# A residual graph kernel: attention as fp16 products on 64x64 tiles, graph sums kept in PSUM, and a mix of three float32r products

## The chip, the cores and the metric

One core of one Trainium2 chip. The metric is the device time of one execution in microseconds, as the median of the runs.

## The reference, cut to what matters

The input is x, 128 batches of 64 rows of 512 float32, and one 64x64 graph `adj` for all batches.

```python
# L0: rows of a batch are mixed by the graph
x = layernorm(x + einsum('bnf,nm->bmf', x, adj * adj) + bias)
# L1: two graphs from two projections, then attention with both
z_l, z_g, v = h @ W_lang.T, h @ W_grav.T, h @ W_V.T          # h is the x above
A_l = relu(zn @ zn.T) * not_eye                  # zn: rows of z_l, normalised
A_g = exp(-max(sq_i + sq_j - 2 z_g @ z_g.T, 0) / (2 sigma**2)) * not_eye
K = w * row_stochastic(A_l * adj) + (1 - w) * row_stochastic(A_g * adj)
out = layernorm(h + (K @ v) @ W_O.T)
```

The result must be close to float32, so the kernel writes most products as three fp16 products (high x high, high x low, low x high).

## The kernel before, in words

The 128 batches are worked in 16 groups of 8 batches (512 rows, as 4 pairs of batches on 128 partitions). All engines run the same software pipeline, written out by hand: one turn handles group g, the group before it (`before`) and the one after it (`nxt`). Turn 0 and turn 15 stand outside the hardware loop, which holds two turns. Each engine runs its own list in order; semaphores join them. I call the start of a turn the moment at which TensorE begins `mix(nxt, 0)`.

TensorE's list in a turn is: `mix` of pairs 0 and 1 of the next group; `project` 0 (12 products); `mix` 2 and 3; `project` 1; `kernel_t` of the group before; `project` 2; four `attend`; `project` 3 to 7; `values` 0; `gram`; `values` 1; `symmetrise`; `values` 2; `spread`; `values` 3. `project` j fills one of three banks; ScalarE rounds it to fp16 (`p_high`, tile `p_hi`) and VectorE takes the rest (`p_low`, tile `p_lo`). From j = 3 on `project` j waits for `p_low` of j - 3.

VectorE's list begins with `similarities` and `gravities` of the group before, then `add_bias` 0 and 1 (tile `y`), `row_factors`, `p_low` 0, `scale_rows` (tile `ks_sb`, which `kernel_t` waits for), `add_bias` 2 and 3, two `row_stats`, `p_low` 1, `row_moments`, four `residual` (tile `o`), `p_low` 2, `norm_rows` (four times tile `h`), and the other `p_low`. ScalarE's list begins with `p_high` 0, `p_high` 1, `kt_copy`, `p_high` 2, three `h_high`, `p_high` 3. GpSimd computes both `rstd`, half of `h_lo`, and `t_diag`.

SyncE issues the loads of `x_in` and the stores of `o` in one queue, in order: a store waits for `out_ready`, which the last `normalise` of the group (tile `o`, ScalarE) completes. Of `x_in` there are two buffers; the load into one waits for the `mix` that read it.

At the end of a turn the graph sums run over VectorE: `sums` adds `ps_t` and `t_sb`, `distances` makes three more passes, and then ScalarE takes the exponential:

```python
dve.tensor_tensor(s_sb[:, :], ps_t[:, :], t_sb[:, :], ALU.add)
...
act.activation(e_sb[GR, :], w_sb[GR, :], ACT.Exp, scale=cexp[GR, 0:1])
```

Of the kernel before, what the change touches and what calls it, by code (L numbers as in the profile page):

```python
# [23 lines left out]
F16 = mybir.dt.float16  # L24
ALU = mybir.AluOpType
# [29 lines left out]
def resnorm_graph_kernel(nc, x, adj, bias, w_lang, w_grav, w_v, w_o, gate, log_sigma, out):  # L55
# [18 lines left out]
    with ctx:  # L74
# [10 lines left out]
        x_in = [sb(f"x_in{i}", [P, PAIRS, D]) for i in range(2)]  # L85
# [8 lines left out]
        u = sb("u", [P, PAIRS, D])  # L94
# [4 lines left out]
        v_diag = sb("v_diag", [P, ROWS])  # L99
        s_sb = sb("s_sb", [P, ROWS])  # L100
        w_sb = sb("w_sb", [P, ROWS])
# [3 lines left out]
        kt = sb("kt", [P, PAIRS, P])  # L105
# [13 lines left out]
        vec = sb("vec", [P, GB])  # L119
# [8 lines left out]
        w_raw["v"] = u  # L128
# [11 lines left out]
        ones_lg = sb("ones_lg", [P, P])  # L140
# [5 lines left out]
        wmix = sb("wmix", [P, P])  # L146
        not_eye = sb("not_eye", [P, N])
# [9 lines left out]
        cexp = sb("cexp", [P, 1])  # L157
        minus_half = sb("minus_half", [P, GB])
# [6 lines left out]
        t_scale = sb("t_scale", [P, 1])  # L165
        wv_scale = sb("wv_scale", [P, 1])
# [7 lines left out]
        ku_bank = [ps_k, *front, ps_k]  # L174
# [43 lines left out]
        u_ready = sem("u_ready")  # L218
# [18 lines left out]
        kt_ready = sem("kt_ready")  # L237
# [87 lines left out]
        def _(pe):  # L325
# [16 lines left out]
            def project(g, j, first):  # L342
# [15 lines left out]
                for n, (k, a, b) in enumerate(passes):  # L358
# [61 lines left out]
            def attend(g, p, mixed):  # L420
# [6 lines left out]
                elif p == 3:  # L427
                    pe.wait_ge(sum_ready, g.count(4, 1))
# [692 lines left out]
```

## Time and profile before

| what | value |
|---|---|
| median of 3 runs | 627.45 us (626.82 to 627.95) |
| span of the profiled execution | 625.0 us |
| median less span | 2.45 us |
| TensorE busy | 614.2 us, 98% of the span |
| VectorE, ScalarE, GpSimd busy | 444.2, 242.7, 155.5 us |
| share of the chain that ended last on TensorE | 96% |
| turns 2 and 3 | start at 112.70 and 148.44 us |

The profile gives the profiled execution by its span; a time of its own with what lies around the span is not in it, and the 2.45 us between the span and the median are taken as that. A busy time is the union of an engine's instructions. A TensorE record of 128x512 fp16 lasts 0.38 us though the next starts 0.216 us later: products overlap, so costs on TensorE are read from starts. A float32 product leaves two records.

### The profile page before, as it was taken

How to read it: one execution, taken by the hardware profiler on the slowest of the kernel's cores; microseconds unless marked ns; L12 is line 12 of the kernel's file. 1: busy time of each engine (PE TensorE's matmuls, PEld its weight loads, DVE VectorE, ACT ScalarE, POOL GpSimd, SP SyncE). 2: the span in 40 equal slices, each digit the busy share in tenths (PEclk: the TensorE clock that was granted, in tenths of full speed). 3: DMA queues.
4: the chain of work that ended last, by engine and by line, in shares of the span. 5: the costliest groups of instructions: out<-in, count | busy, mean ns of one | idle time of the engine just before them, and what ended most of it. 6: DMA issues, size and time to landing. Idle time of an engine off the chain costs nothing.

```text
span 625.0 us, 11961 instructions
## 1 busy us (share of the span) xinstructions
PE 614.2 (98%) x4468; PEld 315.0 (50%) x4468; DVE 444.2 (71%) x940; ACT 242.7 (39%) x413; POOL 155.5 (25%) x159
## 2 busy tenths in 40 slices
PE   9999999999999999999999999999999999999994
PEld 6543545454454545454454545445454545545452
DVE  1759486877868586876868687786858788686564
ACT  2345224333443424434432433344342443443333
POOL 1002205032231403123230503223140312323021
PEclk9999999999999999999999999999999999999999
DMA  8722203434123342423223342312334242302103
GB/s 269 244 44 87 51 1 68 136 53 125 52 62 116 64 134 60 141 42 87 90 50 134 67 134 55 120 51 58 119 67 134 59 143 42 92 17 51 69 2 135
DMA packets 89392, 55.05 MB, mean 88 GB/s; under 512 B 70816, under 2 KB 70816, under 8 KB 89376
## 3 DMA queue, kind: packets, MB, share of 16 engines
q1 hardware_dynamic: 19744, 38.05, 17.9%
q10 hardware_dynamic: 69632, 16.79, 13.4%
q8 instruction: 10, 0.16, 0.1%
q14 instruction: 6, 0.05, 0.0%
HBM read 21.27 MB, written 16.78 MB: 61 GB/s over the span
## 4 chain that ended last, share of the span: by engine, by line
PE 96%; DVE 2%; ACT 1%; POOL 0%; issue 0%; POOLq 0%; ACTq 0%; DVEq 0%
PE proj L359 31%; PE proj L375 27%; PE front L339 9%; PE ps_t L389 7%; PE front L429 4%; PE ps_k L429 4%; PE ps_t L400 3%; PE ps_v L409 2%; PE proj L499 2%; PE proj L529 2%; PE ps_v L416 2%; PE ps_t L499 1%; PE ps_k L329 1%; DVE p_lo L736 1%; PE ps_t L529 1%; DVE y L709 0%
## 5 line engine op out<-in xcount | busy, mean ns | idle before, releaser
L557 ACT ACTIVATE p_hi<-proj 128x512 f16<-128x512 f32 x128 | 75.9, 593 | 118.2 <-PE proj L359 117.7
L736 DVE TENSOR_TENSOR p_lo<-proj,p_hi 128x512 f16<-128x512 f32 x128 | 86.0, 688 | 20.9 <-ACT p_hi L557 17.9
L375 PE MATMUL proj<-m_hi,ht_hi 128*128 128x512 f16 x256 | 97.2, 380 | 0.7 <-DVE p_lo L736 0.7
L375 PE MATMUL proj<-m_hi,ht_lo 128*128 128x512 f16 x256 | 97.0, 379 | 0.0
L375 PE MATMUL proj<-m_lo,ht_hi 128*128 128x512 f16 x256 | 97.0, 379 | 0.0
L1026 POOL TENSOR_TENSOR ve<-mv,eps_ln 128x4 f32<-128x4 f32 x31 | 6.6, 212 | 307.7 <-DVE mv L718 211.5
L562 ACT ACTIVATE u<-proj 128x512 f32<-128x512 f32 x64 | 37.9, 592 | 82.7 <-PE proj L375 82.5
L543 ACT ACTIVATE h_hi<-h 128x512 f16<-128x512 f32 x64 | 36.5, 619 | 69.0 <-DVE h L726 69.0
L1065 POOL TENSOR_TENSOR h_lo<-h,h_hi 128x512 f16<-128x512 f32 x30 | 41.5, 1403 | 84.4 <-ACT h_hi L543 84.4
L359 PE MATMUL proj<-ht_hi,l_grav_hi 128*128 128x512 f16 x160 | 60.6, 379 | 0.6 <-DVE p_lo L736 0.6
L359 PE MATMUL proj<-ht_hi,l_lang_hi 128*128 128x512 f16 x160 | 60.8, 380 | 0.0
L359 PE MATMUL proj<-ht_lo,l_grav_hi 128*128 128x512 f16 x160 | 60.6, 379 | 0.0
L359 PE MATMUL proj<-ht_hi,l_grav_lo 128*128 128x512 f16 x160 | 60.6, 379 | 0.0
L359 PE MATMUL proj<-ht_lo,l_lang_hi 128*128 128x512 f16 x160 | 60.6, 379 | 0.0
L359 PE MATMUL proj<-ht_hi,l_lang_lo 128*128 128x512 f16 x160 | 60.6, 379 | 0.0
L339 PE MATMUL front<-x_in,wmix 128*128 128x512 f32 x128 | 60.2, 593 | 0.0
L593 ACT ACTIVATE o<-o,nmr,rstd 128x512 f32<-128x512 f32 x60 | 46.9, 807 | 9.7 <-issue 9.3
L709 DVE TENSOR_TENSOR y<-front,bias_b 128x512 f32<-128x512 f32 x64 | 42.5, 686 | 11.3 <-PE front L339 10.8
L389 PE MATMUL ps_t<-ht_hi,p_lo 128*128 128x64 f16 x512 | 46.5, 193 | 0.0
L389 PE MATMUL ps_t<-ht_lo,p_hi 128*128 128x64 f16 x512 | 46.5, 193 | 0.0
L389 PE MATMUL ps_t<-ht_hi,p_hi 128*128 128x64 f16 x512 | 46.5, 193 | 0.0
L389 PEld LDWEIGHTS ps_t<-ht_hi,p_hi 128*128 128x128 f16 x512 | 45.1, 98 | 2.3 <-issue 0.5
(166 smaller groups left out, 1051.8 us busy)
## 6 DMA issues: line engine op xcount, KB each, us to landing
x_in<-in_x SPq DMA_DIRECT2D x16, 1024.0 KB, 7.1
out<-o SPq DMA_DIRECT2D x15, 1024.0 KB, 5.0
w_raw_lang<-in_L_gnn_W_lang SPq DMA_DIRECT2D x4, 256.0 KB, 3.1
o<-in_L_gnn_W_O SPq DMA_DIRECT2D x1, 1024.0 KB, 10.2
w_raw_grav<-in_L_gnn_W_grav SPq DMA_DIRECT2D x4, 256.0 KB, 10.1
u<-in_L_gnn_W_V SPq DMA_DIRECT2D x1, 1024.0 KB, 12.0
ht_hi<-h_hi ACTq DMA_TRANSPOSE x64, 2.4
ht_lo<-h_lo ACTq DMA_TRANSPOSE x64, 2.5
```

The costliest lines, as they stand in the source:

```text
L339: pe.matmul(front[p % 2][:, :], wmix[:, :], x_in[g.parity][:, p, :], start=True, stop=True).then_inc(l0_done, 1)
L359: mm = pe.matmul(proj[j % 3][:, :], a[s][:, blk(k, c), :], b[g.parity][:, k, :], start=(n == 0), stop=(n == len(passes) - 1))
L375: mm = pe.matmul(proj[j % 3][:, :], a[g.parity][:, k, p * P:(p + 1) * P], b[:, k, :], start=(n == 0), stop=(n == len(passes) - 1))
L389: mm = pe.matmul(ps_t[:, b * N:(b + 1) * N], a[:, c, b, :, :].rearrange("p s n -> p (s n)"), t[g.parity][:, c, b * N:(b + 1) * N], start=( ...
L429: pe.matmul(ku_bank[p][:, :], kt[:, p, :], u[:, p, :], start=True, stop=True).then_inc(ku_done, 1)
L543: act.activation(h_hi[:, p, :], h[g.parity][:, p, :], ACT.Copy).then_inc(hhi_ready, 1)
L557: act.activation(p_hi[:, j % 4, :, j // 4, :], by_batch(proj[j % 3]), ACT.Copy).then_inc(phi_ready, 1)
L562: act.activation(u[:, p, :], proj[(8 + p) % 3][:, :], ACT.Copy).then_inc(u_ready, 1)
L593: act.activation(o[:, p, :], o[:, p, :], ACT.Identity, scale=rstd2[:, p:p + 1], bias=nmr2[:, p:p + 1]).then_inc(out_ready, 1)
L709: dve.tensor_tensor(y[:, p, :], front[p % 2][:, :], bias_b[:, :], ALU.add).then_inc(y_ready, 1)
L736: dve.tensor_tensor(p_lo[:, j % 4, :, j // 4, :], by_batch(proj[j % 3]), p_hi[:, j % 4, :, j // 4, :], ALU.subtract).then_inc(plo_ready, 1)
L1065: pool.tensor_tensor(h_lo[:, p, :], h[g.next().parity][:, p, :], h_hi[:, p, :], ALU.subtract).then_inc(hlo_ready_pool, 1)
```

## The change

- `mix` becomes three float32r products per pair (`wmix_hi` x `x_hi`, `wmix_lo` x `x_hi`, `wmix_hi` x `x_lo`). ScalarE makes `x_hi` (`x_high`, four copies) and GpSimd `x_lo` (`x_low`, four subtractions), in turn g for group g + 2. There is one `x_in` buffer; its next load waits for `x_low`.
- `attend`: four float32 products become 24 fp16 products with stationary tiles of 64x64, in two halves of 12. `u` and `kt` are split in two fp16 parts each: `u_low` four times and `kt_low` once on VectorE. Before the last product of `project` 2 TensorE waits for `kt_low`, for all `u_low` and for all four `y`.
- `values` uses stationary tiles of 64 columns, 24 products where 12 stood.
- The graph sums: `symmetrise` adds into `ps_t` (8 products where 16 stood), `spread` adds 8 small products after its large one, and `sums` and `distances` go from VectorE. `rectify` and the exponential on ScalarE read PSUM.
- SyncE's order of loads and stores.

```diff
@@ sync @@
             def reload(g):
-                sp.wait_ge(l0_done, g.count(4, 4))
-                load(Group(g.half + 1, g.parity))
+                sp.wait_ge(xlo_ready, g.count(4, 4))
+                load(g.next())
...
-            load(Group(0, 1))
             reload(Group(0, 0))
+            reload(Group(0, 1))
+            reload(Group(1, 0))
+            store(Group(0, 0))
             with sp.Fori(0, G // 2 - 2) as i:
-                reload(Group(i, 1))
-                store(Group(i, 0))
-                reload(Group(i + 1, 0))
+                reload(Group(i + 1, 1))
                 store(Group(i, 1))
+                reload(Group(i + 2, 0))
+                store(Group(i + 1, 0))
@@ tensor @@
-                pe.matmul(front[p % 2][:, :], wmix[:, :], x_in[g.parity][:, p, :],
-                          start=True, stop=True).then_inc(l0_done, 1)
+                passes = ((wmix_hi, x_hi), (wmix_lo, x_hi), (wmix_hi, x_lo))
+                for n, (w, x_part) in enumerate(passes):
+                    mm = pe.matmul(front[p % 2][:, :], w[:, :], x_part[g.parity][:, p, :],
+                                   start=(n == 0), stop=(n == len(passes) - 1))
...
+                pe.matmul(ps_v[:, :], w_spread[:, :], r_sb[:, :],
+                          start=True, stop=True, skip_group_check=True).then_inc(spread_done, 1)
+                for b in range(GB):
+                    mm = pe.matmul(ps_v[GR, b * N:(b + 1) * N], r_sb[:, b * N:(b + 1) * N],
+                                   eye_g[:, :], start=False, stop=True, skip_group_check=True)
...
+            def attend_waits(g, nxt):
+                pe.wait_ge(ktlo_ready, g.count(1, 1))
+                pe.wait_ge(ulo_ready, g.count(4, 4))
+                if nxt:
+                    pe.wait_ge(y_ready, nxt.count(4, 4))
+
+            def attend(g, a, banks, on_residual=()):
+                passes = ((kt_hi, u_hi), (kt_hi, u_lo), (kt_lo, u_hi))
+                for n, (kt, u) in enumerate(passes):
+                    for q in range(2):
+                        half = slice(q * N, (q + 1) * N)
+                        for side in range(2):
+                            mm = pe.matmul(banks[2 * a + q][side * N:(side + 1) * N, :], kt[half, 2 * a + side, :],
+                                           u[half, 2 * a + side, :], start=(n == 0 and 2 * a + q not in on_residual),
+                                           stop=(n == len(passes) - 1))
@@ scalar @@
+            def x_high(g, first=False):
+                act.wait_ge(x_loaded[g.parity], g.half * 16 + 16)
+                if not first:
+                    act.wait_ge(l0_done, g.prev().prev().count(4, 4))
+                for p in range(PAIRS):
+                    act.activation(x_hi[g.parity][:, p, :], x_in[:, p, :], ACT.Copy).then_inc(xhi_ready, 1)
...
+                if split_next and not first:
+                    x_high(nxt.next())
                 p_high(g, 0, first)
@@ vector @@
                 if has_prev:
-                    similarities(before)
+                    u_low(before, 3)
                     gravities(before)
...
                 p_low(g, 1)
+                if has_prev:
+                    kt_low(before)
...
-                sums(g)
-                distances(g)
+                similarities(g)
+                u_low(g, 2)
@@ gpsimd @@
+            def x_low(g):
+                for p in range(PAIRS):
+                    pool.wait_ge(xhi_ready, g.count(4, p + 1))
+                    pool.tensor_tensor(x_lo[g.parity][:, p, :], x_in[:, p, :], x_hi[g.parity][:, p, :],
+                                       ALU.subtract).then_inc(xlo_ready, 1)
```

SyncE's loop over two turns, before, where two loads and two stores take turns and a load waits for `l0_done` (the `mix`):

```order
L268 ISA [waits l0_done]
L268 DMA x_in<-in_x 128x4x512
L271 REGISTER_ALU
L272 ISA [waits out_ready]
L272 DMA out<-o 128x4x512
```

The same place of the changed kernel:

```order
L284 ISA [waits xlo_ready]
L284 DMA x_in<-in_x 128x4x512
L287 ISA
L288 ISA [waits out_ready]
L288 DMA out<-o 128x4x512
```

The pattern is the same, but the load now waits for GpSimd's `x_low`, and by the group numbers in the diff the load of group g + 2 follows the store of group g - 2 in the queue.

ScalarE from the end of one turn into the next, in the loop. Before (`o` is `normalise` of pair 3, `u` is `u_copy` 3, `p_hi` are `p_high` 0 and 1 of the new turn):

```order
L574 ACTIVATE e_sb<-w_sb,cexp 64x512 [waits d2_ready]
L593 ACTIVATE o<-o,nmr,rstd 128x512 [waits nmr2_ready]
L561 REGISTER_ALU
L562 ACTIVATE u<-proj 128x512 [waits proj_done]
L556 ISA [waits gram_done]
L557 ACTIVATE p_hi<-proj 128x8x64 [waits proj_done]
```

Now:

```order
L629 ACTIVATE e_sb<-ps_v,cexp 64x512 [waits d2_done]
L646 ACTIVATE o<-o,nmr,rstd 128x512 [waits nmr2_ready]
L612 REGISTER_ALU
L613 ACTIVATE uv<-proj 128x512 [waits proj_done]
L586 ISA
L590 ACTIVATE x_hi<-x_in 128x512 [waits l0_done,x0_loaded]
L590 ACTIVATE x_hi<-x_in 128x512 x3
L607 ISA [waits gram_done]
L608 ACTIVATE p_hi<-proj 128x8x64 [waits proj_done]
```

Four copies that wait for the load of x have come between the last `u` of a turn and the first `p_hi` of the next.

VectorE from `scale_rows` to the first `residual`, before:

```order
L805 TENSOR_TENSOR ks_sb<-a_sb,cfac 128x512 [waits deg_ready]
L708 REGISTER_ALU
L709 TENSOR_TENSOR y<-front,bias_b 128x512 [waits l0_done]
L708 REGISTER_ALU
L709 TENSOR_TENSOR y<-front,bias_b 128x512 [waits l0_done]
L713 BN_STATS stats<-y 128x6 [waits y_ready] x2
L735 REGISTER_ALU [waits stats1_ready]
L736 TENSOR_TENSOR p_lo<-proj,p_hi 128x8x64 [waits phi_ready]
L718 BN_AGGR mv<-stats 128x2 x4
```

Now:

```order
L863 TENSOR_TENSOR ks_sb<-a_sb,cfac 128x512 [waits deg_ready]
L769 REGISTER_ALU
L770 TENSOR_TENSOR y<-front,bias_b 128x512 [waits l0_done]
L769 REGISTER_ALU
L770 TENSOR_TENSOR y<-front,bias_b 128x512 [waits l0_done]
L774 BN_STATS stats<-y 128x6 [waits y_ready] x2
L806 REGISTER_ALU [waits stats1_ready]
L807 TENSOR_TENSOR p_lo<-proj,p_hi 128x8x64 [waits phi_ready]
L802 TENSOR_TENSOR kt_lo<-ps_v,kt_hi 128x256 [waits kthi_ready]
L779 BN_AGGR mv<-stats 128x2 x4
```

`kt_lo`, for which `attend` waits, stands behind `ks_sb`, two `y`, two `stats` and a `p_lo`.

## Rows read from the trace of the kernel before

**Rows 1.** The page's busy times of each engine.

```profile
PE 614.2 (98%) x4468; PEld 315.0 (50%) x4468; DVE 444.2 (71%) x940; ACT 242.7 (39%) x413; POOL 155.5 (25%) x159
```

**Rows 2.** Timeline, TensorE, turn 2: start, us, engine, line, operation, records.

```profile
112.70 1.88 PE L339 MATMUL front<-x_in,wmix 128*128 128x512 f32 x4
114.42 0.38 PE L359 MATMUL proj<-ht_hi,l_lang_hi 128*128 128x512 f16 x1
...
120.45 0.38 PE L359 MATMUL proj<-ht_hi,l_lang_lo 128*128 128x512 f16 x1
120.76 0.69 PE L416 MATMUL ps_v<-eye,ks_sb 128*64 128x64 f32 x16
...
122.68 1.02 PE L429 MATMUL ps_k<-u,kt 128*128 128x512 f32 x2
...
126.11 0.38 PE L359 MATMUL proj<-ht_hi,l_lang_hi 128*128 128x512 f16 x1
...
131.29 0.38 PE L359 MATMUL proj<-ht_hi,l_grav_hi 128*128 128x512 f16 x1
...
141.31 0.27 PE L400 MATMUL ps_t<-eye_l,t_sb 128*64 128x64 f32 x1
141.32 0.27 PE L400 MATMUL ps_t<-eye_g,t_sb 128*64 128x64 f32 x1
...
142.40 0.39 PE L375 MATMUL proj<-m_hi,ht_hi 128*128 128x512 f16 x1
...
145.00 1.02 PE L409 MATMUL ps_v<-v_diag,ones_lg 128*128 128x512 f32 x2
...
148.44 1.88 PE L339 MATMUL front<-x_in,wmix 128*128 128x512 f32 x4
```

**Rows 3.** Timeline, VectorE, turn 2; in brackets idle time before and its releaser.

```profile
113.94 1.37 DVE L709 TENSOR_TENSOR y<-front,bias_b 128x512 f32<-128x512 f32 x2
...
117.84 0.69 DVE L736 TENSOR_TENSOR p_lo<-proj,p_hi 128x512 f16<-128x512 f32 x1
118.44 0.68 DVE L805 TENSOR_TENSOR ks_sb<-a_sb,cfac 128x512 f32<-128x512 f32 x1
...
123.84 0.69 DVE L811 TENSOR_TENSOR o<-ps_k,h 128x512 f32<-128x512 f32 x1 [1.22 <-PE ps_k L429]
...
127.52 1.91 DVE L726 TENSOR_SCALAR h<-y,mv,rstd 128x512 f32<-128x512 f32 x4
...
130.28 0.69 DVE L736 TENSOR_TENSOR p_lo<-proj,p_hi 128x512 f16<-128x512 f32 x1 [0.25 <-ACT p_hi L557]
```

**Rows 4.** Timeline, ScalarE, turn 2.

```profile
113.22 0.81 ACT L593 ACTIVATE o<-o,nmr,rstd 128x512 f32<-128x512 f32 x1
113.94 0.57 ACT L562 ACTIVATE u<-proj 128x512 f32<-128x512 f32 x1
117.21 0.60 ACT L557 ACTIVATE p_hi<-proj 128x512 f16<-128x512 f32 x1 [2.70 <-PE proj L359]
...
128.09 1.67 ACT L543 ACTIVATE h_hi<-h 128x512 f16<-128x512 f32 x3 [4.62 <-DVE h L726]
```

**Rows 5.** Timeline, SyncE's queue, turn 2.

```profile
114.20 0.41 SPq L272 DMA_DIRECT2D out<-o  x1
114.93 0.39 SPq L268 DMA_DIRECT2D x_in<-in_x  x1
```

**Rows 6.** View of the tile `x_in`: time from issue to landing of its 16 loads.

```profile
DMA to landing us min/median/max: 5.3/7.1/11.0
```

**Rows 7.** Timeline, GpSimd, turn 2.

```profile
139.64 1.27 POOL L1048 TENSOR_TENSOR t_diag<-t_sb,eye 128x512 f32<-128x512 f32 x1 [0.67 <-ACT t_sb L570]
```

**Rows 8.** Timelines of the start: GpSimd, then VectorE.

```profile
45.86 0.55 POOL L1060 TENSOR_TENSOR rnorm<-ssq_all,minus_half 128x1 f32<-128x1 f32 x1 [12.01 <-DVE ssq_all L830]
...
53.25 0.37 DVE L718 BATCH_NORM_AGGREGATE mv<-stats 128x2 f32<-128x6 f32 x4
```

**Rows 9.** TensorE's last products; windows after them (PE, PEld, DVE, ACT, POOL, PEclk, DMA, GB/s).

```profile
616.85 1.02 PE L444 MATMUL proj<-u,kt 128*128 128x512 f32 x2
...
621.00:622.00 1.00, 0.00 (x0) 0.00 (x0) 0.55 (x1) 0.78 (x1) 0.00 (x0) 1.00 0.89 334
622.00:623.00 1.00, 0.00 (x0) 0.00 (x0) 0.00 (x0) 0.00 (x0) 0.00 (x0) 0.56 0.28 106
```

More of the change, by code:

```diff
@@ L24 @@
 F16 = mybir.dt.float16
+F32R = mybir.dt.float32r
 ALU = mybir.AluOpType
@@ L82, in sem @@
             return ctx.enter_context(nc.semaphore(name))
-        x_in = [sb(f"x_in{i}", [P, PAIRS, D]) for i in range(2)]
+        x_in = sb("x_in", [P, PAIRS, D])
+        x_hi = [sb(f"x_hi{i}", [P, PAIRS, D], F32R) for i in range(2)]
+        x_lo = [sb(f"x_lo{i}", [P, PAIRS, D], F32R) for i in range(2)]
         y = sb("y", [P, PAIRS, D])
@@ L358, in project @@
                 for n, (k, a, b) in enumerate(passes):
+                    if attended and n == len(passes) - 1:
+                        attend_waits(*attended)
                     mm = pe.matmul(proj[j % 3][:, :], a[s][:, blk(k, c), :], b[g.parity][:, k, :],
@@ L391, in gram @@
                                        t[g.parity][:, c, b * N:(b + 1) * N],
-                                       start=(n == 0), stop=(n == len(passes) - 1))
+                                       start=(b == 0 and n == 0), stop=(n == len(passes) - 1),
+                                       skip_group_check=True)
                 mm.then_inc(gram_done, 1)
@@ L466, in iteration @@
                     kernel_t(before)
-                project(g, 2, first)
+                project(g, 2, first, (before, nxt) if has_prev else None)
                 if has_prev:
-                    for p in range(PAIRS):
-                        attend(before, p, nxt)
+                    for a in range(2):
+                        attend(before, a, ku_bank)
                 for j in range(3, 7):
@@ L506, in _ @@
             gram_of("lang")
-            pe.wait_ge(dve_const, 3)
+            pe.wait_ge(dve_const, 7)
+            pe.matmul(ps_v[L, 0:N], mask[:, :], eye_l[:, :], start=True, stop=True).then_inc(mask_turned, 1)
+            pe.wait_ge(wmix_ready, 2)
             for p in range(PAIRS):
@@ L611, in iteration @@
                 if first:
+                    x_high(nxt, first=True)
                     m_high(0)
+                if split_next and not first:
+                    x_high(nxt.next())
                 p_high(g, 0, first)
+                if split_next and first:
+                    x_high(nxt.next())
                 if first:
@@ L617, in iteration @@
                 if has_prev:
-                    kt_copy(before)
+                    kt_high(before)
                 p_high(g, 2, first)
@@ L661, in iteration @@
                 if has_next:
-                    exponent(g)
+                    rectify(g)
+                    exponent(g, first)
                 if has_prev:
                     normalise(before, (3,))
-                u_copy(g, 3)
+                u_high(g, 3)
+            x_high(Group(0, 0), first=True)
             for k in range(DC):
@@ L844, in back @@
             def back(g):
-                similarities(g)
+                u_low(g, 3)
                 gravities(g)
@@ L944, in iteration @@
                 diagonals(g)
+                shifted(g)
+                if first or not has_next:
+                    u_low(g, 0)
+                u_low(g, 1)
                 diagonal_matrices(g)
-                sums(g)
-                distances(g)
+                similarities(g)
+                u_low(g, 2)
             dve.memset(ones[:, :], 1.0).then_inc(dve_const, 1)
@@ L1062, in iteration @@
                     ln1(g.next())
+                if split_next and not has_prev:
+                    x_low(g.next().next())
+                if has_next:
                     for p in (2, 3):
```

287 lines of the change are left out of this document (157 added, 130 removed).

## The prediction

> **What bounds the kernel now.** I read the page's busy times first, then the timelines of the engines over one turn, taken from its first `mix`. TensorE is busy for 98% of the span [rows 1]. Turn 2 starts at 112.70 and turn 3 at 148.44, so a turn is 35.74 us, and TensorE's rows have no wait in it [rows 2]. The other engines have gaps and wait for TensorE (ScalarE 2.70 us ahead of `p_hi` 0, VectorE 1.22 us ahead of the first residual) [rows 3, 4]. So TensorE's instruction stream sets the turn. A saving there counts only until a chain on another engine fills the turn; so that chain has to be followed too.
>
> **The change, TensorE alone.** An fp16 product of 512 columns takes 0.216 us: 24 of them lie between 126.11 and 131.29 [rows 2].
> - Mix: a float32 product takes (114.42 - 112.70)/2 = 0.86. No row shows float32r. Its bounds are the fp16 pace, 0.216, and the float32 one, 0.86; one of the two records that a float32 product leaves would be 0.43. I take 0.216, as the fp16 scheme of three products is what it copies: a mix 0.65, four mixes 2.6 where 3.44 stood, -0.85. At 0.43 they would be 5.2, at 0.86 10.3.
> - Attend: four products took 126.11 - 122.68 = 3.43. Now 24 products on quarters of the array. That two products on different column halves run together is shown by `symmetrise`: `eye_l` and `eye_g` start 0.01 us apart, and its 16 pairs of records, from 141.31 to 142.40, come every 0.06 us [rows 2]. If four run together, attend is 6 x 0.216 = 1.3, -2.14. One at a time it is 5.2, two at a time 2.6. I take 1.3, since the pairs in the row do overlap. For the same reason `values` (24 half-wide products) stays at 2.6; were its halves to run one after the other, each turn would grow by 10.4.
> - Graph sums: `symmetrise` keeps its length (the 8 products that go ran beside the 8 that stay). `spread` gets 8 such products more: 16 records at 0.06, +0.95.
> - Narrow and wide tiles in turn: `kernel_t` starts at 120.76 where the product before (120.45) ends its slot at 120.67, so a switch is 0.09 us. A turn had 4, now it has 10: into and out of `values` 0, out of `gram`, round the large product of `spread`, into the next mix, and for attend: +0.55.
>
> The sum is 35.74 - 0.85 - 2.14 + 0.95 + 0.55 = 34.25 us a turn, if nothing else waited.
>
> **What fills the turn instead.** All offsets are from the turn's first mix. Three waits are new.
>
> *First, the load of x.* SyncE's queue now issues the load for group g + 2 behind the store of group g - 2, and that store waits for the last `normalise` in turn g - 1. Before, that `normalise` ended at 113.22 + 0.81 = 114.03 (offset 1.33), as it stood behind an exponential that waited for three VectorE passes [rows 4]. Now the exponential waits for TensorE's `spread` only. From the end of `gram` the list runs: values 1 to 2.7, symmetrise to 3.7, values 2 to 6.3, spread to 8.3, values 3 to 10.9, turn ends at 11.0. On ScalarE: `u` 2 6.5 to 7.1, `normalise` 2 to 7.9, `rectify` to 8.6, exponential to 9.3, `normalise` 3 to 10.15. So it ends 0.85 us ahead of the new turn. The store is issued 0.17 later, the load 0.73 after that [rows 5], and lands after 7.1 us, the median [rows 6]: offset 7.15. ScalarE's four `x_hi` (0.55 each, by the three `h_hi` in 1.67 [rows 4]) wait for it, and `p_hi` 0 stands behind them: 9.35 to 9.95. VectorE's `p_lo` 0 starts at a = 10.0; before at 117.84, offset 5.14 [rows 3]. Behind it are `ks_sb`, for which `kernel_t` waits, and everything else of the turn. TensorE, ready for `kernel_t` at 7.2, idles until a + 1.25 = 11.3.
>
> *Second, `kt_lo`.* VectorE goes at 0.6 us an operation (117.84 to 118.44 [rows 3]): `ks_sb` a + 0.6, `y` a + 1.2 and 1.8, stats a + 2.4 and 3.0, `p_lo` 1 a + 3.6, `kt_lo` a + 4.2 to 4.65 (half the elements of the others, with the fixed part of one). TensorE then does one product, the switch, and attend from a + 5.0.
>
> *Third, what follows from it.* Before, the first residual started 1.16 after attend did (122.68 to 123.84 [rows 2, 3]), which is 0.43 to the product's second record and 0.73 from there. Now the third pass starts 0.43 after attend, and its records are 0.21 shorter: a + 5.0 + 0.43 + 0.73 - 0.21 = a + 5.95. Four residuals at 0.65, `p_lo` 2 a + 8.5, `h` a + 9.1. From `h` (127.52) to `p_lo` 3 (130.28) it is 2.76 [rows 3]: a + 11.85. `project` 6 needs that one and starts at a + 12.6; its own stream would allow a + 11.6. From there to the end of the turn it was 148.44 - 131.29 = 17.15 [rows 2]; now + 0.95 + 0.4 (switches) = 18.5.
>
> So a turn is a + 31.1 = 41.1 us, +5.4. Turns 2 to 13 have this wait (12 turns: +64.8). Where x is there early (turn 1) or not split (turn 14), a comes from VectorE: `u_lo` 3 until 1.4, `gravities` until 2.15, then `y` to `p_lo` 0 as before (117.84 - 113.94 = 3.9 [rows 3]): a = 6.05, turn 37.15, +1.4 each.
>
> **The start.** In the first mix x must be split by ScalarE and GpSimd (1.3 us an operation by `t_diag` [rows 7]), about +1. In turn 0 `x_hi` and `x_lo` of group 1 stand ahead of the `rnorm` on GpSimd (before at 45.86 [rows 8]): four subtractions from about 46.1 to 51.3. The load for group 2 is issued only then and, alone on the queues, should land after the shortest time seen, 5.3 us [rows 6]; `x_hi` of it stands ahead of `p_high` 1. So `mv`, before at 53.25 [rows 8], comes at about 61.3, and the rest of turn 0 follows it: +8.0, with +1.3 for spread and switches: +9.3 in all.
>
> **The end.** The last turn's attend and the final one save 4.3, spread and switches cost 1.3, two waits for `kt_lo` 0.9, and the chain `u_lo` 3, `gravities`, factors, `ks_sb` now starts behind the last values, +3.4: about +1.5.
>
> **Sum:** 627.45 + 9.3 + 1.4 + 64.8 + 1.4 + 1.5 = 705.9; I forecast 706. (The profiled span of 625.0 gives 703.4.)
>
> **A rule weighed.** The idle stretches of TensorE are about 4 us now. In the trace the clock stayed at 1.00 for four and more microseconds after the last product (616.85 to past 622.00) and then fell to the lower level, 0.50 of full speed, in the window 622:623, whose mean is 0.56 [rows 9]. So a gap of 4.1 us may or may not reach a fall. If it does, kernel_t and project 2 at half speed are hidden by the wait for `kt_lo`, attend is 1.3 longer, and project 3 to 5 lose their 1.0 of slack and more: about +2.5 a turn, up to +30, 736. The Trainium skill ("TensorE: Matmul & The Clock Gate", "HAM oscillation") says that idle gaps between bursts of products bring the clock back to half rate, with the next burst then run slowly. By that rule the time would be at the 736 end; by the row the gap is just under what was seen to be survived.
>
> The skill's "TensorEngine Tiling (Array Packing)", "Tiling Modes", says that tiles load weights and multiply in parallel. This would give attend its 1.3; the row shows it for two column tiles with float32, none here for row tiles.
>
> **Rivals.**
> - *x is there in time* (no wait at `x_hi`; SyncE's order costs nothing). For it: before, the loads hid everywhere. Against it: the landing time and the queue's order. Only the `kt_lo` chain is left: 627.45 + 9.3 + 14 x 1.4 + 1.5 = 658. Chance 0.10.
> - *TensorE stays the bound, faster.* A turn is a + 31.1, so it gets under 35.74 only if a is under 4.6, that is if x lands before offset 1.8, 5.3 us earlier than worked out, and `kt_lo` is not waited for. At 34.25 a turn: 627.45 + 9.3 - 14 x 1.5 + 1.5 = 617. Chance 0.11, for an error of mine in the order of the queues above all.
> - *Dearer products.* Float32r at 0.43 hides in the wait ahead of `kernel_t` (4.1 of room, +2.6 needed); at 0.86 it is 3.6 more in 12 turns and 7.7 in the others, 760. Attend two at a time: +1.3 in 15 turns, 726. Values not paired: 706 + 16 x 10.4 = 872. Or the clock falls in every gap, 736. Chance of a time over 740: 0.09.
> - *The forecast*, the wait for x in 12 turns and `kt_lo` in all: 0.68, with a range of its own from 690 (x lands 1.3 us sooner) to 740 (attend or the clock dearer). No change: 0.02.
>
> **Range.** 680 to 740: below it are the first two rivals, above it the dear products, about 2 in 10 with parts of each. A run tells 0.2% from no change; the cases give faster 0.11, within 0.2% 0.02, slower 0.87.
>
> **What would show it.** ScalarE: `x_hi` in turns 2 to 13 waits for the load of x, some 6 us, and `p_hi` 0 starts near offset 9.4. TensorE: `kernel_t` waits about 4 us for `ks_sb`, the last product of project 2 about 1.5 for `kt_lo`, project 6 about 1 for `p_lo` 3. Mixes 0.65 a pair, attend 1.3. I am wrong if the load of x is issued well ahead of the store's wait, if it lands in less than 5 us, or if `values` takes other than 2.6.

## Result, and the profile after

| kernel | median | ratio to before |
|---|---|---|
| before | 627.7 us (626.82 to 628.09, 4 runs) | |
| changed | 740.63 us (740.06 to 741.11, 4 runs) | 1.1802 [1.1786, 1.1819] |

The change costs 113 us. The forecast of 706, slower by three waits, had the three waits in the right places and the first in its size; the second and third, the start and the end were put too small. The time lies 0.6 us above its range. The page of the changed kernel (span, busy times, TensorE's granted clock in 40 slices, the chain that ended last), to be read beside [rows 1]:

```profile
span 738.2 us, 14214 instructions
PE 635.1 (86%) x5558; PEld 353.4 (48%) x5558; DVE 473.4 (64%) x964; ACT 274.8 (37%) x477; POOL 222.8 (30%) x204
PEclk9999999999898999989998999989899998999996
PE 47%; DVE 19%; DMA 12%; ACT 9%; issue 9%; SPq 1%; POOL 1%; DVEq 0%; ACTq 0%; POOLq 0%
```

TensorE had 98% of the span and 96% of the chain. Now it has 47% of the chain, and a DMA, which had nothing, has 12%. The waits (in total, times, longest) name the places:

```profile
ACT x_hi L590 <- DMA x_in<-in_x: 90.5, 14, 9.6
PE ps_v L447 <- DVE ks_sb L863: 61.8, 15, 5.2
PE proj L382 <- DVE p_lo L807: 20.0, 16, 5.3
PE proj L382 <- DVE kt_lo L802: 4.1, 7, 1.6
```

One turn, from its first mix at 216.17. TensorE's timeline (the next turn starts at 259.61, a turn of 43.44):

```profile
216.17 0.50 PE L359 MATMUL front<-x_hi,wmix_hi 128*128 128x512 f32 x1
216.51 0.39 PE L359 MATMUL front<-x_hi,wmix_lo 128*128 128x512 f32 x1
216.74 0.39 PE L359 MATMUL front<-x_lo,wmix_hi 128*128 128x512 f32 x1
...
228.53 1.18 PE L447 MATMUL ps_v<-eye,ks_sb 128*64 128x64 f32 x16 [4.75 <-DVE ks_sb L863]
...
232.07 0.61 PE L382 MATMUL proj<-ht_hi,l_lang_lo 128*128 128x512 f16 x1
232.61 0.64 PE L465 MATMUL ps_k<-uv,kt_hi 64*64 64x512 f16 x2
...
241.00 0.39 PE L382 MATMUL proj<-ht_hi,l_grav_hi 128*128 128x512 f16 x1 [0.60 <-DVE p_lo L807]
```

SyncE's queue, then ScalarE:

```profile
215.39 0.40 SPq L288 DMA_DIRECT2D out<-o  x1
216.37 0.39 SPq L284 DMA_DIRECT2D x_in<-in_x  x1
```

```profile
223.51 2.19 ACT L590 ACTIVATE x_hi<-x_in 128x512 fp32r<-128x512 f32 x4 [6.63 <-DMA x_in<-in_x]
225.60 1.06 ACT L608 ACTIVATE p_hi<-proj 128x512 f16<-128x512 f32 x2
```

VectorE, then GpSimd:

```profile
226.21 0.69 DVE L807 TENSOR_TENSOR p_lo<-proj,p_hi 128x512 f16<-128x512 f32 x1 [4.13 <-ACT p_hi L608]
226.82 1.65 DVE L863 TENSOR_TENSOR ks_sb<-a_sb,cfac 128x512 f32<-128x512 f32 x1
228.40 1.27 DVE L770 TENSOR_TENSOR y<-front,bias_b 128x512 f32<-128x512 f32 x2
...
231.59 0.41 DVE L802 TENSOR_TENSOR kt_lo<-ps_v,kt_hi 128x256 f16<-128x256 f32 x1
...
234.26 0.75 DVE L869 SCALAR_TENSOR_TENSOR o<-ps_k,ku_scale,h 128x512 f32<-128x512 f32 x1 [1.96 <-PE front L465]
...
240.25 0.69 DVE L807 TENSOR_TENSOR p_lo<-proj,p_hi 128x512 f16<-128x512 f32 x1 [0.25 <-ACT p_hi L608]
```

```profile
224.21 5.39 POOL L1116 TENSOR_TENSOR x_lo<-x_in,x_hi 128x512 fp32r<-128x512 f32 x4 [13.74 <-ACT x_hi L590]
```

Read it as the chain runs. The load of x is issued at 216.37, behind the store; ScalarE stands 6.63 us; `p_lo` 0 starts at offset 10.04 (forecast a = 10.0); `kernel_t` waits 4.75. Two things are not in the forecast's sum. `ks_sb` takes 1.65 where it took 0.6 to 0.7, beside GpSimd's `x_lo`. And the windows of TensorE (busy, count, granted clock) show the clock at the lower level when `kernel_t` starts, until attend is nearly done:

```profile
227.00:228.00 1.00, 0.00 (x0) 0.94 0.00 0
228.00:229.00 1.00, 0.47 (x8) 0.50 0.00 0
...
234.00:235.00 1.00, 1.00 (x16) 0.64 0.00 0
```

The clock fell in each of turns 2 to 13, from about 2.6 us ahead of `kernel_t` to 0.5 after its start. The turn shown is one of the longest: from `p_lo` 0 to `project` 6 it has 14.79, the ten turns have 13.93 to 14.81, 14.37 in the mean.

`ks_sb` of turn k marks the turns. The 113.2 us between the spans divide as: start, to the first `ks_sb`, +17.1 (99.80 against 82.70); turns 1 to 13 together +88.2; the last two turns and the end +7.9. The forecast had 9.3, 66.2 and 2.9, so 7.8, 22.0 and 5.0 were missing. The mean of ten full turns is 43.04, forecast 41.1.

### The profile page after: what moved, and what is told of

Same layout as the page of the kernel before. It is cut to its first block, busy times and chain, and to the rows that moved or that the text cites. A ratio compares the mean times of both kernels' runs of the same rounds, so it can differ in the third digit from the quotient of the medians.

```text
span 738.2 us, 14214 instructions
## 1 busy us (share of the span) xinstructions
PE 635.1 (86%) x5558; PEld 353.4 (48%) x5558; DVE 473.4 (64%) x964; ACT 274.8 (37%) x477; POOL 222.8 (30%) x204
## 4 chain that ended last, share of the span: by engine, by line
PE 47%; DVE 19%; DMA 12%; ACT 9%; issue 9%; SPq 1%; POOL 1%; DVEq 0%; ACTq 0%; POOLq 0%
PE proj L400 19%; DMA x_in<-in_x 12%; PE proj L382 7%; PE ps_t L414 6%; DVE p_lo L807 3%; DVE o L869 3%; ACT x_hi L590 3%; DVE ks_sb L863 3%; PE ps_v L435 2%; DVE y L770 2%; PE ps_v L438 2%; DVE stats L774 2%; PE ps_k L465 2%; ACT p_hi L608 2%; PE ps_t L425 2%
## 5 line engine op out<-in xcount | busy, mean ns | idle before, releaser
L1116 POOL TENSOR_TENSOR x_lo<-x_in,x_hi 128x512 fp32r<-128x512 f32 x64 | 85.6, 1370 | 192.4 <-ACT x_hi L590 192.4
L400 PE MATMUL proj<-m_hi,ht_hi 128*64 128x512 f16 x512 | 122.5, 384 | 0.0
L400 PE MATMUL proj<-m_lo,ht_hi 128*64 128x512 f16 x512 | 120.7, 379 | 0.0
L400 PE MATMUL proj<-m_hi,ht_lo 128*64 128x512 f16 x512 | 120.6, 379 | 0.0
L613 ACT ACTIVATE uv<-proj 128x512 f16<-128x512 f32 x64 | 38.2, 597 | 99.3 <-PE proj L400 99.3
L797 DVE TENSOR_TENSOR uv<-proj,uv 128x512 f16<-128x512 f32 x64 | 43.7, 684 | 44.7 <-ACT uv L613 44.2
L447 PE MATMUL ps_v<-eye,ks_sb 128*64 128x64 f32 x256 | 16.7, 296 | 61.8 <-DVE ks_sb L863 61.8
L590 ACT ACTIVATE x_hi<-x_in 128x512 fp32r<-128x512 f32 x64 | 35.0, 617 | 90.5 <-DMA x_in<-in_x 90.5
L382 PE MATMUL proj<-ht_lo,l_grav_hi 128*128 128x512 f16 x160 | 61.3, 383 | 0.0
L400 PEld LDWEIGHTS proj<-m_hi,ht_hi 128*64 128x64 f16 x512 | 43.0, 110 | 23.4 <-DVE p_lo L807 5.9
L400 PEld LDWEIGHTS proj<-m_hi,ht_lo 128*64 128x64 f16 x512 | 43.2, 110 | 21.4 <-issue 0.2
```

Of the source, the lines that this page charges most:

```text
L382: mm = pe.matmul(proj[j % 3][:, :], a[s][:, blk(k, c), :], b[g.parity][:, k, :], start=(n == 0), stop=(n == len(passes) - 1))
L400: mm = pe.matmul(proj[j % 3][q * N:(q + 1) * N, :], a[g.parity][:, k, rows:rows + N], b[:, k, :], start=(n == 0), stop=(n == len(passes) - 1))
L590: act.activation(x_hi[g.parity][:, p, :], x_in[:, p, :], ACT.Copy).then_inc(xhi_ready, 1)
L613: act.activation(u_hi[:, p, :], proj[(8 + p) % 3][:, :], ACT.Copy).then_inc(uhi_ready, 1)
L797: dve.tensor_tensor(u_lo[:, p, :], proj[(8 + p) % 3][:, :], u_hi[:, p, :], ALU.subtract).then_inc(ulo_ready, 1)
L1116: pool.tensor_tensor(x_lo[g.parity][:, p, :], x_in[:, p, :], x_hi[g.parity][:, p, :], ALU.subtract).then_inc(xlo_ready, 1)
```

## The experiments

Medians of 4 runs beside before on the same chip (627.7 to 628.2), turns as the mean of ten from the starts of `ks_sb`. The theory from the traces: (1) the place of the load behind the store, (2) where `kt_lo` and `p_lo` 3 stand in VectorE's list, (3) GpSimd's `x_lo` holding VectorE up, (4) the clock falling in the gap. Rivals: that the products themselves are dearer, or that the operand splits are too long a chain in any order.

**1. The load one place earlier.**

```diff
             reload(Group(1, 0))
+            reload(Group(1, 1))
             store(Group(0, 0))
-            with sp.Fori(0, G // 2 - 2) as i:
-                reload(Group(i + 1, 1))
-                store(Group(i, 1))
+            with sp.Fori(0, G // 2 - 3) as i:
                 reload(Group(i + 2, 0))
+                store(Group(i, 1))
+                reload(Group(i + 2, 1))
                 store(Group(i + 1, 0))
...
```

> SyncE issues each load of x before the store that it stood behind; nothing else is changed. Theory 1 (the load's place in the queue makes x_hi wait 6.6 us and sets the turn): the wait at x_hi goes, p_lo 0 starts near 6 us after the first mix and not 10, the turn falls from 43.0 to 37.2 and the time from 740.6 to about 671. Theory 2 (x_lo on GpSimd holds up VectorE's operations with two SBUF inputs, so that ks_sb takes 1.65 us and not 0.68, wherever they meet): x_lo now runs from 1.4 to 6.8 us of the turn, beside gravities, the factors and ks_sb, and each may lose up to 1.3 us: p_lo 0 at 7 to 9 us, turn 38 to 40, time 680 to 705. Rival (the turn is bound elsewhere): 735 to 741.

Measured: 700.23 us, ratio 1.1155 [1.113, 1.118], turn 39.42. The wait for x is gone, and the other two stand alone. VectorE, GpSimd and TensorE of a turn:

```profile
370.57 1.67 DVE L838 SCALAR_TENSOR_TENSOR a_sb<-e_sb,mask 64x512 f32<-64x512 f32 x1
372.27 1.29 DVE L772 TENSOR_TENSOR y<-front,bias_b 128x512 f32<-128x512 f32 x2
...
374.67 1.20 DVE L852 TENSOR_TENSOR degr<-deg,rr 128x8 f32<-128x8 f32 x1
```

```profile
370.41 5.43 POOL L1118 TENSOR_TENSOR x_lo<-x_in,x_hi 128x512 fp32r<-128x512 f32 x4 [7.00 <-ACT x_hi L592]
```

```profile
381.84 0.39 PE L384 MATMUL proj<-ht_hi,l_lang_lo 128*128 128x512 f16 x1 [1.62 <-DVE kt_lo L804]
...
389.91 0.39 PE L384 MATMUL proj<-ht_hi,l_grav_hi 128*128 128x512 f16 x1 [0.97 <-DVE p_lo L809]
```

GpSimd's `x_lo` moved with x, and what it meets moved too: now `gravities` takes 1.67 (0.69 in the changed kernel, at 217.63) and `degr`, 8 elements wide, 1.20 (0.15 there). `ks_sb` is back at 0.68. `p_lo` 0 starts 7.87 after the first mix; in run 4, without `x_lo`, it is 5.82. So the hold-up costs 2.0 us a turn in this place, and it is as much as the turn is longer than run 4's (39.42 against 37.45).

**2. GpSimd's `x_lo` on 64 of 512 columns** (the rest of `x_lo` is zero, so the mix lacks that part).

```diff
-                    pool.tensor_tensor(x_lo[g.parity][:, p, :], x_in[:, p, :], x_hi[g.parity][:, p, :],
+                    pool.tensor_tensor(x_lo[g.parity][:, p, 0:64], x_in[:, p, 0:64], x_hi[g.parity][:, p, 0:64],
...
```

> The low part of x is computed for the first 64 of 512 columns only (the rest is zero), so that GpSimd is done before ks_sb; this leaves out part of the mix's correction. Theory 2 (ks_sb is held up by GpSimd's x_lo): ks_sb takes 0.68 us in every turn, 1.0 less in 12 turns: 729. If the gap ahead of kernel_t, 4.9 us now and 3.9 then, no longer brings the clock down, 1.1 to 1.3 a turn more: 713 to 716. Rival (ks_sb is long for a reason of its own): 740.

Measured: 720.45 us (717.39 to 723.40), ratio 1.146 [1.142, 1.151]. `ks_sb` takes 0.68 in every turn, the turn is 42.33 (-0.71), and the first `ks_sb` is at 91.66 in place of 99.80. So 8.1 us of the start are GpSimd's `x_lo` (10.5 in run 5, whose first `ks_sb` is at 89.29). The time lies between the two that I had named, 729 and 713 to 716. The clock still falls in these turns, so the -0.71 is not the price of `ks_sb` alone; run 5 tells that.

**3. The gap filled with 20 fp16 products** ahead of `kernel_t` in turns 1 to 13 (their result is overwritten).

```diff
+            def warm(g):
+                pe.wait_ge(sim_ready, g.count(1, 1))
+                for n in range(20):
+                    pe.matmul(ps_v[:, :], m_hi[:, 0, 0:P], m_hi[:, 1, :], start=True, stop=True)
...
+                    if split_next:
+                        warm(before)
                     kernel_t(before)
```

> 20 fp16 products of 512 columns (4.3 us), whose result is never read, stand ahead of kernel_t in turns 1 to 13. Theory 3 (the clock falls in the gap, and kernel_t, project 2 and attend run at half speed): granted clock 1.0 in these turns, kernel_t 0.6 and not 1.2 us, attend 1.3 and not 2.4, turn 43.0 to about 41.8, less 14 us in all but up to 4 us more in turn 1, which has no gap: 727 to 731. Rival (the slow products are hidden behind the wait for kt_lo): 741 to 745.

Measured: 737.84 us, ratio 1.175 [1.172, 1.177]; mean clock 0.983 in place of 0.941. The clock holds, attend takes 1.4 us in place of 2.4, from `p_lo` 0 to `project` 6 it is 13.94 in every turn in place of 14.37 in the mean, and the turn is 42.61 (-0.43). Over the twelve turns that is 5 us; in all it is 3, since turn 1 gets longer and the first `ks_sb` is 2.2 later in this trace. I had expected 10 to 14: in three of the ten turns the slow products stood wholly in time that the wait for `kt_lo` took anyway, and in none did they cost more than 0.9.

**4. The float32 mix of before** with two `x_in` and before's order of loads and stores; attention and graph sums stay changed.

```diff
-                passes = ((wmix_hi, x_hi), (wmix_lo, x_hi), (wmix_hi, x_lo))
...
+                pe.matmul(front[p % 2][:, :], wmix[:, :], x_in[g.parity][:, p, :],
+                          start=True, stop=True).then_inc(l0_done, 1)
```

> The mix is the float32 product of before with two x_in buffers and the SyncE order of before; attention and graph sums stay changed. Theory 1: all of the loss at the start and in turns 2 to 13 goes; what is left is the chain from u_lo 3 over p_lo 0 and kt_lo to project 6, turn 37.2 against 35.74: time about 650. Rival (the split x is not what costs; attention or values do): over 700. Rival (kt_lo and the chain are hidden as well): TensorE's sum, 35.1 a turn, 619.

Measured: 660.49 us, ratio 1.052 [1.050, 1.054], turn 37.45. The turn is as expected (37.2), the time 10 above the 650 that I had given with it. Without any split of x the two later waits remain, about 1.6 us a turn. TensorE's waits:

```profile
PE proj L377 <- DVE p_lo L788: 14.1, 15, 1.0
PE proj L377 <- DVE kt_lo L783: 9.3, 14, 0.7
```

**5. Runs 2 and 3 in one.** 

> The changed kernel with x_lo on 64 of 512 columns and the gap ahead of kernel_t filled with 20 fp16 products in turns 1 to 13: both terms that the forecast left out, at once. If these two are all of the 1.94 us by which a turn was longer than forecast, and add up, the turn is 43.04 - 0.85 - 0.45 = 41.7 or somewhat less, down to the forecast's 41.1, with the first ks_sb at about 91.7 and the time at 715 to 718. If they hide one another (the load of x sets the pace whatever stands behind it), it stays at 42.2 and 720.

Measured: 718.91 us, ratio 1.145 [1.143, 1.147], turn 41.70. Together the two give -1.34, a little more than their sum (-0.71, -0.43). From `p_lo` 0 to `project` 6 it is now 12.95; with the clock held and `ks_sb` long (run 3) it was 13.94. So the long `ks_sb` costs 1.0 us a turn, and the clock the other 0.4. What is left to the forecast's 41.1 is 0.6.

**6. A new order of VectorE's and ScalarE's lists**, on the float32 mix, on the kernel of run 1, and on that kernel with `x_lo` on VectorE. Its core:

```diff
                     row_factors(before, nxt)
+                    scale_rows(before)
                     p_low(g, 0)
-                    scale_rows(before)
...
                     for p in (2, 3):
                         add_bias(nxt, p)
+                if has_prev:
+                    kt_low(before)
+                if has_next:
                     for p in (2, 3):
                         row_stats(nxt, p)
...
                 p_low(g, 2)
+                p_low(g, 3)
                 if has_next:
                     norm_rows(nxt, before)
+                p_low(g, 4)
```

> The version with the plain float32 mix (660.5 us, turn 37.45), with VectorE's and ScalarE's lists put in another order: kt_lo straight behind the last two y, p_lo 3 ahead of the four h, ks_sb ahead of p_lo 0, gravities at the end of the turn before, and in the last turn the factors ahead of u_lo 2 and 3. No operation is added or dropped. Theory A (the two waits for kt_lo and for p_lo 3 come from where these stand in VectorE's list): both go, the turn falls to TensorE's own sum, 35.1 to 35.5, and the time is about 630 (626 to 638). Theory B (the split of the attention operands is a chain that no order shortens): the turn stays at or above 36.4, the time at or above 645.

> The version with the loads of x one place earlier (700.2 us, turn 39.42), with the new order of VectorE's and ScalarE's lists alone; x_hi and x_lo stay where they are, at the turn's start and on GpSimd. If the kt_lo and p_lo 3 waits are order alone, they go (1.6 and 1.0 us a turn) and what GpSimd's x_lo holds up on VectorE (about 1 us a turn) stays: turn 36.5 to 37.6, time 660 to 675. If x_lo holds up nothing, the turn is at 35 and the time at 640; if the order buys nothing here, 39 and over 690.

> The changed kernel with all three float32r products, with the loads of x issued one place earlier, the same new order of VectorE's and ScalarE's lists, and x_lo subtracted by VectorE in its idle places late in the turn in place of by GpSimd at the turn's start (x_hi late in the turn too). If nothing but the load, GpSimd's x_lo and the two orders cost the time, TensorE's own sum is left: 34.25 by the forecast, 34.4 to 34.8 with 0.23 a float32r product; the first ks_sb at 86 to 89, and 620 in all (612 to 630), which is below the kernel before. If VectorE with 2.4 us more a turn becomes the bound, the turn is over 36 and the time over 645.

Measured: 686.50 (1.093 [1.090, 1.095], 26 us worse than run 4), 688.63 (1.097 [1.095, 1.098]) and 680.71 (1.084 [1.082, 1.086]), turns of 39.9, 39.1 and 39.5. All three missed. The waits for `kt_lo` and `p_lo` 3 went, as meant, but another came: I had put `p_hi` 5 on ScalarE behind a wait for `h_lo`. TensorE, VectorE and GpSimd of the first:

```profile
381.86 0.64 PE L395 MATMUL proj<-m_hi,ht_hi 128*64 128x512 f16 x2 [2.64 <-DVE p_lo L786]
```

```profile
378.04 3.16 DVE L771 TENSOR_TENSOR h_lo<-h,h_hi 128x512 f16<-128x512 f32 x2
```

```profile
377.94 2.71 POOL L1133 TENSOR_TENSOR h_lo<-h,h_hi 128x512 f16<-128x512 f32 x2 [4.67 <-ACT h_hi L581]
```

Two `h_lo` on VectorE that take 0.6 to 0.7 each take 3.16, beside GpSimd's own two. And in this gap of 2.64 us the clock fell (windows of TensorE; the last product before it starts at 378.84):

```profile
380.00:381.00 1.00, 0.00 (x0) 1.00 0.01 3
381.00:382.00 1.00, 0.14 (x2) 0.87 0.63 128
382.00:383.00 1.00, 1.00 (x6) 0.50 0.63 130
```

This trace has the same gap in 14 turns. Around ten of them the clock fell, and those turns take 40.1 to 40.9; around the gaps that end at 223.00, 342.72, 502.55 and 622.00 it stayed at 1.00, and the first three of these turns take 39.15. So a fall costs about 1.1 us a turn here, and the ten, by my estimate, 11 of the 26.

**7. One edit of that order alone:** `kt_lo` ahead of the last two row statistics and of `p_lo` 1, on the kernel of run 4. 

> The version with the plain float32 mix (660.5 us, turn 37.45) with one edit: kt_lo ahead of the last two row statistics and of p_lo 1. The wait for kt_lo shrinks by about 0.9 us, to where kt_hi is done. If the third wait of the prediction (residuals, h, p_lo 3, project 6) is what sets the turn, VectorE reaches the first residual only 0.2 us earlier, since the two statistics and p_lo 1 now stand between: turn 37.2 to 37.3, time 657 to 658, and the wait for p_lo 3 longer by what kt_lo's lost. If the wait for kt_lo sets the turn, it falls by 0.9 to 1.3, to 36.2 to 36.5, and the time to 643 to 648.

Measured: 658.85 us, ratio 1.049 [1.047, 1.051], turn 37.31. As expected: one wait shorter, the next longer by nearly as much.

**8. A second order:** `p_hi` 5 and `p_lo` 5 ahead of `h_lo`, and the transposes spread out.

> The plain float32 mix with the first new order (686.5 us, turn 40.2) mended: that order had put p_hi 5 of ScalarE behind a wait for h_lo, and h_lo 0 and 1 of VectorE ahead of p_lo 5, so that values 0 waited 2.6 us a turn. Now p_hi 5 and p_lo 5 stand ahead of them, p_hi 6 and 7 ahead of the first transposes, and the transposes are spread over the rest of the turn. If that was the only new wait, the turn is TensorE's own sum, 35.1 to 35.6, and the time 626 to 636, beside 627.7 before. If the order only moves the wait on to the next bank, the turn stays over 37 and the time over 650.

> The changed kernel with the three float32r products, the loads one place earlier, x_lo on VectorE (one subtraction ahead of the output statistics, one while spread runs, two at the turn's end), x_hi on ScalarE behind p_hi 2, and the same second order. TensorE's own sum is 34.4 to 34.8 a turn; with a wait of some tenths for what GpSimd and VectorE take from one another, 34.4 to 35.3. First ks_sb at about 85.4, so 612 to 628 in all. If the wait only moves on, over 37 and over 650.

Measured: 653.70 (1.041 [1.039, 1.043]) and 654.81 (1.042 [1.040, 1.044]), turns of 37.64 and (nine of ten) 37.62. Missed again: the wait had moved to the end of the turn. TensorE's `spread` and GpSimd in the first:

```profile
413.11 1.10 PE L430 MATMUL ps_v<-r_sb,w_spread 128*128 128x512 f32 x2 [1.25 <-issue]
```

```profile
406.84 1.01 POOL L1092 TENSOR_TENSOR rstd<-ve,minus_half 128x4 f32<-128x4 f32 x1
407.82 1.27 POOL L1113 TENSOR_TENSOR t_diag<-t_sb,eye 128x512 f32<-128x512 f32 x1
```

`t_sb` was there at 406.3; `t_diag` started 1.5 later, behind `rstd`, which nobody needed yet.

**9. A third order:** GpSimd makes `t_diag` and `rr` before `rstd`, ScalarE's `normalise` comes behind the exponential, and small moves of `p_lo` 2 and `p_hi` 6.

```diff
-                if has_prev:
-                    ln2(g.prev())
                 if has_next:
                     t_diagonal(g)
                 inverse_norm(g)
+                if has_prev:
+                    ln2(g.prev())
```

> The plain float32 mix with a third order. In the second (653.7 us, turn 37.64) TensorE waited 0.27 us a turn for p_lo 2, 0.41 for p_lo 7 ahead of gram and 1.25 for r_sb ahead of spread, since GpSimd took rstd ahead of t_diag and VectorE stood at nmr behind it. Now GpSimd makes t_diag and rr first and rstd last, VectorE nmr behind r_sb, p_lo 2 stands ahead of the last residual, p_hi 6 ahead of the wait for h_lo, and ScalarE's normalise behind the exponential. If TensorE's sum is what is left: 37.64 - 1.93 = 35.7 a turn, the same as before the change, and 628 to 634 in all. If a further chain fills it, 36.3 or more a turn and 637 or more.

> The three float32r products, loads one place earlier, x_lo on VectorE, and the third order. From the second (654.8 us, turn 37.62, waits of 0.27, 0.41 and 1.84): 35.1 a turn if TensorE's sum is what is left, 0.6 below the kernel before and 0.6 below the float32 mix, with 621 to 627 in all; this would show that the change has a gain on TensorE of 0.6 us a turn and not the 1.5 of the forecast. If a further chain fills it, 36 or more a turn and over 635.

Measured: with the float32 mix **627.17 us** (10 runs), ratio 0.9992 [0.9983, 1.0002], turn 35.67. With the three float32r products, the load one place earlier and `x_lo` on VectorE **618.50 us** (617.86 to 620.18), ratio 0.9865 [0.9847, 0.9884], turn 35.03. The second is 9.4 us (1.3%) faster than the kernel before, its interval clear of 1, and 2.5 us under the 621 to 627 that I had expected. Its page, and 120 us in one window (TensorE busy, granted clock):

```profile
span 616.0 us, 14206 instructions
PE 601.8 (98%) x5558; PEld 342.5 (56%) x5558; DVE 502.7 (82%) x1028; ACT 275.4 (45%) x477; POOL 140.9 (23%) x140
```

```profile
360.00:480.00 120.00, 119.84 (x1112) 1.00 0.35 96
```

TensorE has next to no wait in a turn here: only its products at 377.11 and 377.54 are 0.43 apart in place of 0.22, as VectorE's `p_lo` of 376.81 ends between them. So the last two traces are the first to show the changed products' own sum, with 0.2 us of a chain on top. A turn of the last one, TensorE:

```profile
359.83 0.50 PE L361 MATMUL front<-x_hi,wmix_hi 128*128 128x512 f32 x1
...
365.31 0.39 PE L384 MATMUL proj<-ht_hi,l_lang_hi 128*128 128x512 f16 x1
...
369.42 0.40 PE L467 MATMUL ps_k<-uv,kt_hi 64*64 64x512 f16 x2
...
370.84 0.39 PE L384 MATMUL proj<-ht_hi,l_lang_hi 128*128 128x512 f16 x1
...
390.14 1.13 PE L437 MATMUL ps_v<-r_sb,w_spread 128*128 128x512 f32 x2
...
391.95 0.40 PE L402 MATMUL proj<-m_hi,ht_hi 128*64 128x512 f16 x1
```

## Why the prediction missed, step by step

The mechanism was right, and three terms were too small: the second wait (`kt_lo` at a + 5.0, in truth a + 6.3 in the mean), the start (+9.3, in truth +17.1) and the end (+1.5, in truth +6.7). One reason stands behind most of the first two: GpSimd's `x_lo` holds up VectorE, which the forecast put at nothing.

**TensorE alone, 34.25 a turn: 35.03.** The products cost more than I took. From starts in the turn at 359.83 of the last run, against [rows 2] and these two of the kernel before:

```profile
118.72 0.38 PE L359 MATMUL proj<-ht_hi,l_lang_hi 128*128 128x512 f16 x1
...
145.85 0.38 PE L375 MATMUL proj<-m_hi,ht_hi 128*128 128x512 f16 x1
```

Mixes and `project` 0 take 5.48 where 6.02 stood (-0.54, forecast -0.85 without its switches; twelve float32r products start every 0.23 us and not 0.216, and 0.1 is lost at the first); attend 1.42 where 3.43 stood (-2.01, forecast -2.14); `spread` up to the start of the next values 1.81 where 0.85 stood (+0.96, forecast +0.95); all else +0.88, of which the forecast had its switches, 0.55, and not the 0.2 for `p_lo`. The sum is -0.71, forecast -1.49. The two mixes of run 9 divide it: 35.74 to 35.67 for attention and graph sums together, 35.67 to 35.03 for the float32r mix. The gain of the fp16 attention, 2.0, is all but eaten by `spread`, by changes of tile and by the 0.2.

**First wait, the load of x: right.** a = 10.04 against 10.0 (10.02 in the mean of ten turns). Run 1 takes it away with 3.6 us a turn and 40 in all.

**Second wait, `kt_lo` at a + 5.0: the term that was mis-sized.** TensorE started attend at a + 6.40. The step that failed is the length of `ks_sb`, which I took at the 0.6 us of every VectorE operation: it takes 1.65, since I gave GpSimd's `x_lo` a length and a place but no effect on VectorE, whose operation came right beside it. Runs 2, 3 and 5 show it, at 1.0 us a turn (in the turns of run 1 the same hold-up lies on `gravities` and `degr`, at 2.0). Another 0.2 lies between the two `stats` and `p_lo` 1: the kernel before already has 3.80 us from `p_lo` 0 to `p_lo` 1 (117.84 to 121.64), and I took 3.6. The last 0.2 is the product and the switch ahead of attend at the lower clock.

The page "SBUF — State Buffer" of the Trainium skill, section "Who interferes with whom", states it: VectorE and GpSimd share a port pair that one holds for a whole instruction, and a VectorE operation with at most one SBUF input, outside the fast modes, is not touched. The rows agree: `y` and `p_lo`, with one input in PSUM, keep their 0.6 to 0.7 beside `x_lo`, while `ks_sb`, `gravities`, `degr` and `h_lo`, with both in SBUF, do not. `h`, with one SBUF tensor as input, is held up too (below); it takes 0.48 us each time alone, less than `y`, so it may be in such a mode, which no run here tests.

**Third wait, `project` 6 at a + 12.6: a + 14.8.** Beyond the 1.4 just told, 0.7 came from attend at the lower clock in the turn shown (first residual 1.65 after attend, forecast 0.95; 1.00 in the turns in which the clock was back by then). The forecast had this as a rival ("the clock falls in every gap"), at 2.5 us a turn; it did fall in every gap, but run 3 gives it 0.43 a turn on the mean, 3 us in all. Slow products behind a wait cost only what sticks out of the next wait. The forecast had set one row against the rival, the clock's stay at 1.00 after the last product of the kernel before [rows 9]; one case was too little, as the gaps of run 6 show.

The Trainium skill ("TensorE: Matmul & The Clock Gate", "HAM oscillation") says that idle gaps between bursts of products bring the lower clock; the trace agrees: the clock fell in or just behind each of the twelve gaps ahead of `kernel_t`.

Runs 4, 7 and 8 show that the second and third waits are links of one ring. Taking one away alone gave 0.1 us (run 7).

**The remainder of 18.5: right** (18.6). Turns come to 43.04 against 41.1: 1.34 are `x_lo` and the clock together (run 5). Of the 0.6 left, 0.35 lie between `p_lo` 0 and `project` 6 (12.95 in run 5, forecast 12.6), 0.2 of it in the gap behind `stats` told above, and 0.1 in the remainder.

**The start, +9.3: +17.1 at the first `ks_sb`.** I had `x_lo` as four operations that delay a small one, and up to `mv` that was right (60.87, forecast 61.3). The rest came behind it. VectorE's four `h` are held for 5.70 us where they take 1.92 in the kernel before (at 55.44), TensorE then waits 5.27 for a `p_lo` and starts again at the lower clock, and in turn 1 `gravities` and `degr` are held for 2.2 more:

```profile
63.06 5.70 DVE L787 TENSOR_SCALAR h<-y,mv,rstd 128x512 f32<-128x512 f32 x4 [0.59 <-POOL rstd L1111]
```

```profile
63.00 5.49 POOL L1116 TENSOR_TENSOR x_lo<-x_in,x_hi 128x512 fp32r<-128x512 f32 x4
```

Run 2 gets 8.1 of it back, run 5 10.5.

**The end, +1.5: about +6.7**, measured between the last two `ks_sb` (37.06 against 30.41; 35.5 in runs 2, 3 and 4): in the last turn `r_sb` stands behind two `u_lo`, `spread` waits 2.06 for it, ahead of `u_lo` 3, `gravities` and the factors, and the clock falls as it starts (0.79 in the window 712 to 713, 0.50 in 713 to 716):

```profile
712.27 1.75 PE L435 MATMUL ps_v<-r_sb,w_spread 128*128 128x512 f32 x2 [2.06 <-issue]
```

With the factors ahead of `u_lo` 2 and 3 in run 9 these last two are 28.1 apart.

**Rivals.** *x is there in time*, 658: run 4 is that case without the split, 660.5. *TensorE stays the bound, faster*, 617: not this kernel, but it is where the last run arrives (618.5), after edits to SyncE's, ScalarE's, VectorE's and GpSimd's lists and with `x_lo` moved, and not by an error in the queue's order. That the numbers are so near is chance: the turn is 0.8 dearer than in that sum, and the first `ks_sb` is 1.8 later than before and not 9.3. *Dearer products*: float32r at 0.23, attend's four tiles and the halves of `values` together as taken; none was dear. *The clock falls in every gap*, 736: it did, at 0.4 us a turn and not 2.5; that the time lies near this number is chance too.

## What to carry to other kernels

When a change puts new operations on the helpers of a kernel that one engine bounds, write down the whole list of each helper and what each bank waits for; the 113 us came from order and from who does the work, and went with them (740.6 to 618.5 with the same arithmetic). Expect a removed wait to come back at the next bank of the ring until all of them are looked at: three orders were needed, and the first was worse than none. A GpSimd operation over two SBUF tensors cost VectorE about 1 us for each operation that it met there, however small: give it the stretches in which VectorE reads PSUM, or give the work to VectorE. And a fall of the clock costs what no later wait hides: 0.4 us a turn here, 1.1 in run 6.

## What the runs showed of the hardware that I had not expected

- A float32r product of 512 columns starts every 0.23 us; a float32 one takes 0.86.
- A VectorE operation on 8 elements took 1.20 us in place of 0.15 beside a GpSimd subtraction.
- The length of a gap did not say whether the clock falls, nor when. Of 14 gaps of 2.64 us in run 6's first kernel ten had a fall, from 0.1 us ahead of the gap's end to 1.3 behind it, and four had none. In the changed kernel the lower level came 2.6 to 5.1 us after the last product, in the kernel before 5.0 [rows 9].
- Twelve pairs of 64-column products in `values` and four 64x64 products at once in attend keep the pace of one full product, 0.216, but each change of tile shape costs about 0.1 us on either side; a turn has ten.
